# Copying attention scores to all 128 rows: spreading matmul replaced by exchanged row halves and an addition

## The reference

```python
q = hidden_states @ Wq.T + bq            # one query row per batch element
k = key_value_states @ Wk.T + bk         # 2048 rows per batch element, 512 wide
v = key_value_states @ Wv.T + bv
q = q / sqrt(32)                         # 16 heads of 32
scores = einsum('bhqd,bhkd->bhqk', q, k)[:, :, 0, :]
attn = clip(scores, 0.0, 1.0)
context = attn[..., None] * v
output = context.reshape(B, K, H * Dh) @ Wo.T + bo
x = x + output
```

## Time and profile before

| | us |
|---|---|
| median of 3 runs (range) | 187.91 (187.72 to 188.17) |
| the profiled execution, device time | 188.1 |
| its span in the trace | 186.3 |
| PE busy | 182.5 (98%), 811 matmuls |
| PE weight loads busy | 149.1 (80%) |
| DVE busy | 168.8 (91%), 186 instructions |
| ACT busy | 115.4 (62%), 158 instructions |
| TensorE's granted clock | full (1.0) for the whole span |

### The profile page before, as it was taken

The page is one execution under the profiler, slowest core; times in us unless marked ns, Lnnn a source line. Parts: engine busy times, 40 slices in busy tenths (PEclk is TensorE's granted clock), DMA queues, the critical chain, the costliest instruction groups (busy, mean ns, idle before and its releaser), DMA issues.

```text
span 186.3 us, 2377 instructions
## 1 busy us (share of the span) xinstructions
PE 182.5 (98%) x811; PEld 149.1 (80%) x811; DVE 168.8 (91%) x186; ACT 115.4 (62%) x158; POOL 14.7 (8%) x21
## 2 busy tenths in 40 slices
PE   8999999999999999999999999999999999999993
PEld 2788878878878888888888888888888888888883
DVE  0799998999999999999999999998997899799763
ACT  3589873977469685745388574862686574775200
POOL 8000000000000010021000010111000010111000
PEclk9999999999999999999999999999999999999999
DMA  5999910006600006289992006299920007289795
GB/s 218 340 388 425 408 62 2 0 0 193 253 10 0 0 0 116 113 126 230 246 421 106 0 0 116 113 134 296 246 115 0 0 0 116 113 127 279 157 369 194
DMA packets 8075, 28.09 MB, mean 151 GB/s; under 512 B 897, under 2 KB 1281, under 8 KB 7937
## 3 DMA queue, kind: packets, MB, share of 16 engines
q1 hardware_dynamic: 6336, 21.67, 30.4%
q0 software_dynamic: 1728, 6.29, 19.9%
HBM read 19.57 MB, written 8.39 MB: 150 GB/s over the span
## 4 chain that ended last, share of the span: by engine, by line
PE 96%; DMA 2%; ACT 0%; DVE 0%; issue 0%
PE bank_y L337 9%; PE bank_y L341 9%; PE bank_y L339 9%; PE bank_x L337 8%; PE bank_x L341 8%; PE bank_x L339 8%; PE bank_z L341 6%; PE bank_z L339 6%; PE bank_z L337 6%; PE bank_x L415 4%; PE score_bank L397 4%; PE score_bank L396 4%; PE bank_z L415 3%; PE bank_x L433 2%; DMA work<-first_t 2%; PE bank_y L415 1%
## 5 line engine op out<-in xcount | busy, mean ns | idle before, releaser
L574 ACT CAST form_hi<-work 128x1024 fp32r<-128x1024 f32 x28 | 29.0, 1051 | 24.6 <-PE score_bank L397 11.5
L850 DVE TENSOR_TENSOR form_lo<-work,form_hi 128x1024 fp32r<-128x1024 f32 (+1 forms) x38 | 40.2, 1077 | 4.3 <-ACT form_hi L574 4.3
L609 ACT ACTIVATE work<-bank_y,const 128x512 f32<-128x512 f32 x30 | 19.9, 688 | 9.6 <-PE bank_y L341 9.6
L831 POOL DMA_DIRECT2D work<-x_t x12 | 10.5, 875 | 150.7 <-DVE work L885 144.4
L337 PE MATMUL bank_x<-form_hi,wo_hi 128*128 128x512 f32 x52 | 20.3, 390 | 0.0
L339 PE MATMUL bank_x<-form_lo,wo_hi 128*128 128x512 f32 x52 | 20.2, 389 | 0.0
L341 PE MATMUL bank_x<-form_hi,wo_lo 128*128 128x512 f32 x52 | 20.2, 389 | 0.0
L609 ACT ACTIVATE work<-bank_x,const 128x512 f32<-128x512 f32 x24 | 16.0, 686 | 5.3 <-PE bank_x L341 5.3
L874 DVE SCALAR_TENSOR_TENSOR work<-relu,work 128x1024 f32<-128x1024 f32 x16 | 19.1, 1217 | 0.0
L337 PE MATMUL bank_y<-form_hi,wv_hi 128*128 128x512 f32 x48 | 18.8, 391 | 0.0
L341 PE MATMUL bank_y<-form_hi,wv_lo 128*128 128x512 f32 x48 | 18.7, 389 | 0.0
(11 more groups left out here) (153 smaller groups left out, 393.9 us busy)
## 6 DMA issues: line engine op xcount, KB each, us to landing
x_raw<-x_t SPq DMA_DIRECT2D x16, 512.0 KB, 7.0
out_t<-work SPq DMA_DIRECT2D x14, 512.0 KB, 3.3
work<-x_t POOLq DMA_DIRECT2D x12, 512.0 KB, 5.6
work<-first_t SPq DMA_DIRECT2D x2, 512.0 KB, 3.8
work<-wq_t SPq DMA_DIRECT2D x2, 512.0 KB, 8.7
work<-wk_t SPq DMA_DIRECT2D x2, 512.0 KB, 11.2
work<-wo_t SPq DMA_DIRECT2D x1, 1024.0 KB, 13.6
out_t<-work SPq DMA_DIRECT2D x3, 256.0 KB, 2.0
```

The source lines that it names most:

```text
L574: nc.scalar.copy(flat(form_hi, kind), raw(kind, phase)).then_inc(hi_ready[kind], 1)
L609: nc.scalar.activation(result_set(phase)[:, q, j * ROWS:(j + 1) * ROWS], of[:, j, :], ACT.Identity, bias=bias[:, tile:tile + 1], scale=sca ...
L831: pool.dma_start(output_set(s)[:, q, :], x_t[s, q], accum_op=ALU.add).then_inc(residual_added[q], 16)
L850: return nc.vector.tensor_tensor(to, of, hi.bitcast(F32), ALU.subtract)
```

## The change

- `a_for_hi` and `a_for_lo` have all 128 columns filled: columns 0 to 63 hold each head's rounded part four times, columns 64 to 127 of `a_for_hi` hold the remainders four times, and those of `a_for_lo` are zero. The eight score matmuls stay as they are in number and shape, and leave one part of each score on 64 rows of the bank and the other part on the other 64.
- `round_scores`, `split_scores`, `spread` and the `select` matrix are gone. ACT copies the bank to SBUF (`copy_scores` to `score_rows`), SP issues two transfers per half group (`swap_scores`), each of 64 rows x 512 float32 (128 KB), which bring the other half of the rows into `score_others`, and DVE adds the two (`sum_scores`). `relu_scores` now reads SBUF.
- Which output column stands on which row is laid out anew on the host (`by_value_tile`), and one block of Wo's parts (S4) now shares its home with the operands of the opening that `score_hi` and `score_parts` held, with a wait on each engine.
- The hand-written lists of ACT and DVE are in another order throughout; on PE `scores(s, 1)` stands one block product earlier from group 1 on, and scores wait for `score_copied` instead of `relu_ready`.

```diff
-            def spread(s, half):
-                pe.wait_ge(score_parts_ready, score_number(s, half) + 1)
-                pe.matmul(score_bank[half][:, :], select[:, :], score_parts[:, :], start=True, stop=True).then_inc(spread_done, 1)
...
-                wait(pe, relu_ready, score_number(s, half) - 1)
+                wait(pe, score_copied, score_number(s, half) - 1)
...
+            def swap_scores(s, half):
+                sp.wait_ge(score_copied, score_number(s, half) + 1)
+                wait(sp, scores_summed, score_number(s, half) - 1)
+                for to, of in ((0, SIDE), (SIDE, 0)):
+                    sp.dma_start(score_others[to:to + SIDE, half, :],
+                                 score_rows[of:of + SIDE, half, :]).then_inc(scores_swapped[half], 16)
...
-            def round_scores(s, half):
+            def copy_scores(s, half):
                 act.wait_ge(score_done, score_number(s, half) + 1)
-                wait(act, score_parts_ready, score_number(s, half))
-                nc.scalar.copy(score_hi[:, :], score_bank[half][:, :]).then_inc(score_hi_ready, 1)
+                wait(act, relu_ready, score_number(s, half) - 1)
+                nc.scalar.copy(score_rows[:, half, :], score_bank[half][:, :]).then_inc(score_copied, 1)
...
-            def split_scores(s, half):
-                number = score_number(s, half)
-                dve.wait_ge(score_hi_ready, number + 1)
-                wait(dve, spread_done, number)
-                nc.vector.scalar_tensor_tensor(
-                    out=score_parts[:, :], in0=score_hi[:, :].bitcast(F32), scalar=const[:, C_LO:C_LO + 1],
-                    in1=score_bank[half][:, :], op0=ALU.mult, op1=ALU.add).then_inc(score_parts_ready, 1)
+            def sum_scores(s, half):
+                dve.wait_ge(scores_swapped[half], 32 * (s + 1))
+                nc.vector.tensor_tensor(score_rows[:, half, :], score_rows[:, half, :], score_others[:, half, :],
+                                        ALU.add).then_inc(scores_summed, 1)
...
-                twice = of.unsqueeze(2).to_broadcast([P, 6, 2, HEADS])
+                copies = of.unsqueeze(3).to_broadcast([P, 6, HEADS, COPIES])
```

More of the change, by code:

```diff
@@ L17 @@
 ROWS = 512
-REP = P // HEADS
 SUPERS = 4
@@ L568, in hi @@
                     act.wait_ge(a_rows_done, 1)
-                elif before == VALUES and kind in FIRST_PHASE_KINDS:
+                elif before == VALUES and kind in FIRST_PHASE_KINDS and (kind != B22 or s_before == 0):
                     act.wait_ge(score_done, score_number(s_before, kind in (T3, B22)) + 1)
@@ L635, in relu_scores @@
                 b = s // 2
-                nc.scalar.activation(relu[:, half, :], score_bank[half][:, :], ACT.Relu,
+                nc.scalar.activation(relu[:, half, :], score_rows[:, half, :], ACT.Relu,
                                      bias=c_score[:, b:b + 1]).then_inc(relu_ready, 1)
@@ L696, in wo_sum_part @@
                 act.wait_ge(wo_sum_ready[n], 1)
+                if form == S4:
+                    act.wait_ge(q_rows_done, 1)
                 nc.scalar.copy(flat(wo_hi, form), wblock(wo_sums, n)).then_inc(wo_hi_ready[form], 1)
@@ L1240, in _ @@
             add_out22(4)
+            lo(T2, 5)
+            x_t3(5)
+            sum_scores(2, 0)
+            x_t4(5)
             lo(T3, 5)
-            lo(T2, 5)
-            x_t4(5)
+            context(2, Q11)
+            add_out12(4)
+            lo(T4, 5)
+            add_out11(5)
+            sum_scores(2, 1)
+            lo(B11, 6)
+            context(2, Q12)
+            lo(B22, 5)
+            context_t1(6)
             context(2, Q21)
             context(2, Q22)
-            lo(T4, 5)
-            add_out12(4)
-            lo(B22, 5)
-            add_out11(5)
-            lo(B11, 6)
-            split_scores(3, 0)
-            context_t1(6)
+            lo(T1, 6)
             lo(B21, 6)
+            add_out22(5)
+            context_t2(6)
             context_t3(6)
-            lo(T1, 6)
-            context_t2(6)
-            add_out22(5)
             lo(T2, 6)
+            sum_scores(3, 0)
+            context_t4(6)
+            lo(T3, 6)
             context(3, Q11)
-            context_t4(6)
+            lo(T4, 6)
+            add_out12(5)
             lo(B11, 7)
-            context(3, Q21)
-            add_out12(5)
-            lo(T4, 6)
-            split_scores(3, 1)
-            lo(T3, 6)
+            sum_scores(3, 1)
             add_out11(6)
+            context(3, Q12)
             lo(B22, 6)
-            lo(B21, 7)
-            context(3, Q12)
             context_t1(7)
@@ L1273, in _ @@
             lo(T1, 7)
+            add_out22(6)
             context_t2(7)
-            add_out22(6)
+            context(3, Q21)
+            context_t3(7)
             lo(T2, 7)
-            context_t3(7)
+            lo(B21, 7)
             context_t4(7)
             lo(T3, 7)
-            add_x(Q11)
             add_out12(6)
             lo(T4, 7)
+            add_x(Q11)
             lo(B22, 7)
+            add_out11(7)
             add_x(Q12)
-            add_out11(7)
             add_x(Q22)
@@ L1298, in constant_columns @@
     p = np.arange(P)
-    head = p // REP
-    for first in (ROW_HI, ROW_LO, ROW_SMALL):
-        const[first:first + HEADS, C_SELECT:C_SELECT + P] = np.arange(HEADS)[:, None] == head[None, :]
+    head = p % SIDE // COPIES
     const[:, C_SAME:C_SAME + P] = head[:, None] == head[None, :]
     const[:, C_HEAD:C_HEAD + HEADS] = head[:, None] == np.arange(HEADS)[None, :]
-    const[ROW_LO:ROW_LO + HEADS, C_LO] = -1.0
     for first in (0, BATCH * HEADS):
```

205 lines of the change are left out of this document (100 added, 105 removed).

## The result

| | before | after |
|---|---|---|
| median (range), us | 187.91 (187.72 to 188.17) | 186.11 (186.03 to 186.25) |
| profiled execution's span, us | 186.3 | 184.3 |
| matmuls | 811 | 803 |

The ratio is 0.9904, with a 95% interval of 0.9887 to 0.9921: 1.8 us less (1.5 to 2.1). The forecast was 186.0.

A forecast was written before the change was run, and what follows sets the result against it. PE, following itself for 96% of the chain of waits, was taken as the bound. 1.81 us for eight matmuls plus 0.13 for the first stall gave 1.94 us off 187.91: 186.0 us, range 185.6 to 186.9.

The forecast's parts named there:

- Eight matmuls at the step: On PE: eight spreading matmuls go, each worth its step of 0.227 us, 1.81 us in all.
- The stall at B11 of phase 1: PE's late start at B11 of phase 1 goes, as DVE's lo part comes 0.35 to 0.7 us earlier: 0.13 us.
- low bound: On DVE: filling a_for_hi and a_for_lo takes at least 0.5 us longer, by size at the casts' present rate.
- The stall at B11 of phase 2: PE's late start at B11 of phase 2 stays, ACT and DVE reaching it idle as before: 0.
- Leads: DVE ahead of PE: smallest leads 1.2 us at B22 of phase 2 and 1.3 us at T2 of phase 7.
- Everywhere else I find 2 us or more: Leads in places other than B22 of phase 2 and T2 of phase 7 are at least 2 us.
- Transfers: SP's swaps take 2.0 to 2.5 us with nothing queued ahead, up to 7.0 behind loads; cost 0.
- The room of the last pair: Last swap, scores(3, 1): issued at 144.9, its addition reached at 150.1, leaving 5.2 us.
- A: DVE becomes the bound in places: two or three stops cost 0.5 to 1.3 us, 186.5 to 187.3 us; chance 0.13.
- B: Later phases are bound by DVE's list, the eight matmuls' time turns to waiting: 187.9 us; chance 0.05.
- C: Last swap lands late, taking over 8.4 us; at 11.2 us PE stops 4.7 us: 190.7 us; chance 0.04.

The follow-up runs named there:

- the late swaps: Changed kernel with three waited small transfers ahead of the last swap alone: 189.09 us; also rerun with copy_u2(6) ahead of relu_scores(3, 1): 188.18 us.
- the halves: Changed kernel with ACT and DVE making B11's parts of phase 2 in two halves of 512 columns: 185.7 us, repeated 185.62 us.

## Why the prediction was right

**Eight matmuls at the step.** Forecast 1.81 us; putting them back cost 1.80. The Trainium skill's spacing of 131 ns ("TensorE: Matmul & The Clock Gate", section "Back-to-back issue gap") would have made it 1.05; the runs speak for the traced 0.227 us.

**The stall at B11 of phase 1** was to go for 0.13 us: it went (1.92 - 1.80 = 0.12), and moving the two instructions back brought it again, larger. Filling the score operand took this (timeline of DVE, against the earlier trace rows):

```profile
31.01 0.36 DVE L1092 CAST a_for_hi<-a_full 128x384 fp32r<-128x384 f32 x1
...
31.55 0.55 DVE L858 TENSOR_TENSOR a_for_hi<-a_full,a_for_hi 128x384 fp32r<-128x384 f32 x1
```

From 31.01 to 32.10 it is 1.09 us instead of 0.60, the low bound of 0.5 us more.

**The stall at B11 of phase 2** stayed, as forecast. What I did not see is that the new list was needed to keep it from growing: with the old one it grows by 0.40 us. I had written that ACT and DVE reach this place idle "as before". For DVE that was a misreading of the kernel before: its lo part started at 51.50, straight behind two `context` instructions. Only in the new list is DVE idle there. The term of 0 came out right because the list had been changed, not by the argument given.

**Leads.** add_out22(2) against B22 of phase 2: expected to end by 77.5, PE at 78.74. Measured (DVE, PE):

```profile
76.29 1.22 DVE L891 TENSOR_TENSOR work<-bank_z,work 128x1024 f32<-128x1024 f32 x1
```

```profile
78.58 0.39 PE L354 MATMUL bank_z<-form_hi,wo_hi 128*128 128x512 f32 x1
```

It ends at 77.51, lead 1.07; PE came there a little earlier than forecast by the opening's 0.2 us. lo(T2) of phase 7 was expected to end at 163.6, PE at 164.9; measured 163.36 and 164.71, lead 1.35 (DVE, PE):

```profile
162.14 1.22 DVE L858 TENSOR_TENSOR form_lo<-work,form_hi 128x1024 fp32r<-128x1024 f32 x1
```

```profile
164.71 0.39 PE L354 MATMUL bank_y<-form_hi,wo_hi 128*128 128x512 f32 x1
```

"Everywhere else I find 2 us or more" was wrong. I counted leads along DVE's list and PE's, not through ACT's; the way addition, cut-off, copy of U2, T3 of phase 6 has 1.2 us, the smallest that the late swaps brought to light. It cost nothing here, which the prediction had not checked: that was luck.

**Transfers.** 2.0 to 2.5 us each were taken; the median was 2.3. The pair queued behind four loads (issued at 94.3) took up to 8.3; "up to 7.0" was too low, with 25 us of room. The room of the last pair was 5.2 us from issue to addition, as forecast (144.77 to 150.03). "DMA: Bandwidth & Descriptors" of the Trainium skill, section "Rules for kernel authors", advises one transfer of 128 rows instead of two halves since these serialize. Here each half landed 2.3 us after its own issue, as did one transfer of double size: the pair lands later by one issue of SP, about 0.5 us, some 2.8 in all, and not 4.0 as the prediction read that rule. Whether the data of the two halves move one after the other, no run here shows. The prediction also has a slip in this place: 4.0 us would have taken 2.0 us of the room away and left 1.2.

**Rivals.** A (DVE becomes the bound in places) did not occur, but was nearer than 0.13 made it look: one more DVE instruction of 0.6 us per half group costs 2.3 us. B did not occur. C needed a last swap of over 8.4 us; with 8.5 (from the end of ACT's copy at 144.75 to the addition at 153.29) the steady part was 0.3 us longer than before. So its price was right in the steady part; its way, through ACT, was not foreseen, nor were the 1.9 us that half of the executions lost beside it at a lower granted clock.

## What to carry to other kernels

When an engine follows itself through the whole chain of waits, an instruction taken off it is worth its step between starts, and the only further question is whether the other engines' lists still deliver: reorder them with the removal, or part of the gain stays behind (0.40 of 1.92 us here). Count leads through every in-order list between the late thing and the bound engine, the copying engine's above all. When the second engine's records cover 99% of the time, expect anything added to it to show: one instruction of 0.6 us per half group took back the whole gain here. A small saving on the first, the 0.17 us of the halves, still came through; how much more would, was not tried.

## What the runs showed of the hardware

The steady part repeats to 0.01 us between profiled executions of kernels that should not differ; what scatters among them is the opening. Four profiles with the same instructions ahead of the first score matmul (the changed kernel again, waited transfers ahead of all swaps, one transfer, halves again) have it at 33.02, 33.11, 32.57 and 32.40 us. PE's first real matmuls, two in a row each, in the kernel with two instructions ahead and then in the kernel with one transfer:

```profile
4.72 1.19 PE L447 MATMUL bank_x<-form_hi,wv_hi 128*128 128x512 f32 x2
5.71 1.05 PE L447 MATMUL bank_x<-form_hi,wv_lo 128*128 128x512 f32 x2
6.56 0.73 PE L447 MATMUL bank_x<-form_lo,wv_hi 128*128 128x512 f32 x2
```

```profile
4.95 0.70 PE L445 MATMUL bank_x<-form_hi,wv_hi 128*128 128x512 f32 x2 [0.21 <-ACT form_hi L676]
5.49 0.62 PE L445 MATMUL bank_x<-form_hi,wv_lo 128*128 128x512 f32 x2
```

In the first a pair takes 0.85 us (from 5.71 to 6.56) and only from 6.8 us on the usual 0.45; in the second a pair takes 0.54 (from 4.95 to 5.49) and the next ones 0.46. The trace's own records of the granted clock, which the views do not print one by one, put its rise to full at 6.78 and 4.56 us; in both, PE begins with the same nine warm-up matmuls. So the "full for the whole span" of the table of the kernel before holds from its rise on, at 6.33 us there. In the twelve profiles that have such a record the rise lies between 3.66 and 6.78 us, and for the changed kernel itself it was 6.15 in one execution and 4.99 in the other: it varies between executions of one program, and I found nothing in these kernels that sets it. An early rise is not always a gain: in some profiles PE then stops for 0.2 to 0.4 us near 24.5 us, before the products with Wk, for a part of DVE's, and the changed kernel's two openings end within 0.05 us of each other (33.07 and 33.02). Whether more or longer warm-up work would make the rise early every time was not tried.
